# Queries and keys on all partitions in a width-one attention, and large products in two waits at its entry

## The reference

```python
    x = x + _L1_xattn_ref(_layernorm(x, axis=-1), ctx_1024, ...)
    x = x + _L1_ffn_ref(_layernorm(x, axis=-1), ...)
    x = x + _L2_attn_ref(_layernorm(x, axis=-1), L2_attn_w_qkv, L2_attn_w_out)
...
def _L2_attn_ref(x, w_qkv, w_out):
    DIM_HEADS = 64
    b, n, _ = x.shape
    h = DIM_HEADS
    qkv = jnp.einsum('bnc,fc->bnf', x, w_qkv)
    q, k, v = jnp.split(qkv, 3, axis=-1)
    q = q.transpose(0, 2, 1)[..., None]
    k = k.transpose(0, 2, 1)[..., None]
    v = v.transpose(0, 2, 1)[..., None]
    scale = 1.0 / jnp.sqrt(jnp.float32(h))
    dots = jnp.einsum('bhid,bhjd->bhij', q, k) * scale
    causal = jnp.tril(jnp.ones((n, n), dtype=bool))
    dots = jnp.where(causal, dots, -jnp.inf)
    attn = jax.nn.softmax(dots, axis=-1)
    out = jnp.einsum('bhij,bhjd->bhid', attn, v)
    out = out[..., 0].transpose(0, 2, 1)
    return jnp.einsum('bnh,ch->bnc', out, w_out)
```

## Time and profile before

| | |
|---|---|
| median of 3 runs | 3169.06 us (3167.29 to 3172.32) |
| the profiled execution | 3174.21 us, span 3172.4 us |
| TensorE busy | 2943.1 us, 93% |
| VectorE, ScalarE, GpSimd busy | 1863.2, 1253.7, 432.8 us |
| DMA | 37.75 MB, mean 12 GB/s |
| width-one stage, first scores to last values | about 1757 to 2032 us |
| mean granted clock of TensorE | 0.967 |

### The profile page before, as it was taken

How to read it: one execution, slowest core, us unless ns; L and a number is a source line. 1 busy time by engine, 2 the same in 40 slices (tenths; PEclk the granted TensorE clock), 3 DMA queues, 4 the chain that set the end, 5 groups by cost and what they waited for, 6 DMA issues and landing times.

```text
span 3172.4 us, 52215 instructions
## 1 busy us (share of the span) xinstructions
PE 2943.1 (93%) x20631; PEld 1958.4 (62%) x20671; DVE 1863.2 (59%) x6438; ACT 1253.7 (40%) x1944; POOL 432.8 (14%) x458
## 2 busy tenths in 40 slices
PE   7999999988989889988998899999999999998998
PEld 4666666865555556655655556566667766766653
DVE  5534443699999537775677788584343344434455
ACT  2222221335656433324443578554232333323443
POOL 0010010114343311000000256310000000000000
PEclk9999999998999999999999799899999999998999
DMA  3000000010000100000000111100000000000000
GB/s 129 1 1 0 1 0 1 1 52 1 2 1 2 34 32 1 1 5 1 2 1 1 27 36 26 44 2 27 1 1 1 1 1 1 1 1 9 2 1 27
DMA packets 22028, 37.75 MB, mean 12 GB/s; under 512 B 2132, under 2 KB 19733, under 8 KB 20760
## 3 DMA queue, kind: packets, MB, share of 16 engines
q1 hardware_dynamic: 20968, 34.02, 3.2%
q10 hardware_dynamic: 816, 0.39, 0.1%
HBM read 26.81 MB, written 2.10 MB: 9 GB/s over the span
## 4 chain that ended last, share of the span: by engine, by line
PE 77%; DVE 16%; ACT 4%; issue 2%; DMA 0%; DVEq 0%; SPq 0%; POOL 0%; ACTq 0%; POOLq 0%
PE ps L415 45%; DVE arena L568 4%; PE ps L620 2%; PE ps L3040 2%; PE ps L3059 2%; PE ps L686 2%; PE ps L516 2%; ACT arena L674 2%; PE ps L2356 2%; PE ps L1590 2%; PE ps L2310 2%; PE ps L727 2%; DVE arena L1924 2%; PE ps L2913 1%; PE ps L553 1%
## 5 line engine op out<-in xcount | busy, mean ns | idle before, releaser
L415 PE MATMUL ps<-weights,arena 128*128 128x256 f32 (+4 forms) x2480 | 696.1, 430 | 38.9 <-DVE arena L1805 23.5
L415 PEld LDWEIGHTS ps<-weights,arena 128*128 128x128 f32 (+1 forms) x2480 | 462.8, 196 | 204.0 <-issue 94.3
L415 PE MATMUL ps<-arena,weights 128*128 128x256 f32 (+4 forms) x1726 | 560.4, 473 | 14.5 <-DMA weights<-in_w_L_attn 5.8
L415 PEld LDWEIGHTS ps<-arena,weights 128*128 128x128 f32 (+1 forms) x1726 | 316.7, 191 | 217.7 <-issue 154.0
L415 PE MATMUL ps<-arena 128*128 128x256 f32 (+4 forms) x1618 | 429.1, 418 | 6.0 <-ACT arena L4758 1.5
L415 PEld LDWEIGHTS ps<-arena 128*128 128x128 f32 (+2 forms) x1618 | 300.1, 189 | 115.6 <-issue 74.9
L568 DVE TENSOR_REDUCE arena<-ps 128x16 f32<-128x1232 f32 (+2 forms) x96 | 179.1, 1865 | 145.4 <-PE ps L546 48.0
L674 ACT ACTIVATE arena<-ps 77x2048 f32<-77x2048 f32 (+1 forms) x112 | 210.0, 1875 | 120.2 <-PE ps L620 58.4
L1924 DVE MATCH_REPLACE8 arena<-arena 128x77 f32<-128x77 f32 x1024 | 214.3, 224 | 0.0
L2323 ACT ACTIVATE arena<-ps 128x1536 f32<-128x1536 f32 x128 | 185.7, 1451 | 56.6 <-PE ps L2312 49.7
L855 POOL TENSOR_TENSOR x<-x,weights 128x512 f32<-128x512 f32 x32 | 43.8, 1370 | 1201.0 <-DVE arena L821 1153.3
(11 more groups left out here) (427 smaller groups left out, 4421.5 us busy)
## 6 DMA issues: line engine op xcount, KB each, us to landing
arena<-arena SPq DMA_DIRECT2D x156, 32.0 KB
weights<-in_w_L_ffn SPq DMA_DIRECT2D x1, 3848.0 KB, 11.6
weights<-in_w_L_attn SPq DMA_DIRECT2D x1, 3840.0 KB, 14.8
weights<-in_w_L_xattn SPq DMA_DIRECT2D x3, 1024.0 KB, 6.3
weights<-in_w_L_ffn SPq DMA_DIRECT2D x1, 3072.0 KB, 9.9
x<-in_x SPq DMA_DIRECT2D x2, 1024.0 KB
weights<-in_w_L_xattn SPq DMA_DIRECT2D x1, 2048.0 KB, 7.5
out<-x SPq DMA_DIRECT2D x8, 256.0 KB, 2.2
```

The lines of the kernel that those rows point to most:

```text
L415: ins = k.nc.tensor.matmul(out, lhsT, rhs, start=start and i == 0, stop=i == n - 1)
```

## The change

Three things change.

Queries and keys of a batch stand on all 128 partitions: queries on 0 to 63, keys on 64 to 127, 256 columns each, where both stood on 0 to 63 side by side. The bound (which stood behind them on 64 partitions) is laid on both halves, 128 queries each. All operations that cut into parts are therefore 128x384 and not 64x768, the copy from PSUM is 128x256 and not 64x512, the minimum of the bound is written by two operations. For the bound rows there are two transfers a part and not one, so a batch has 24 and not 21; for the first batch the upper half is SyncE's.

The product itself stays in two pieces of 64 columns of weights for batches 0 to 4, the second now written to partitions 64 to 127, and becomes one of 128 columns from batch 5 on (APART). The steps of the bound are put at groups 9, 13, 13, 14, 15 from round 2 on, and not at 9, 10, 13, 13, 14.

TensorE gets nine products of 128x512 in float32 that nothing reads (`awake_tensor`): four in the last step of L1_xattn into bank 2, ahead of the transposed scores, and five in round 0 at g == 2 into bank 0, behind a wait for the exponential of group 1 and ahead of the wait for `left`'s means.

```diff
--- before.py
+++ after.py
@@ -727,6 +727,12 @@
             ins = k.nc.tensor.transpose(out[:, (2 * c + t) * P:(2 * c + t + 1) * P], src[:, t, c * P:(c + 1) * P],
                                         k.ident[:, :])
     return ins
+
+
+def awake_tensor(k, b, n):
+
+    for _ in range(n):
+        k.nc.tensor.matmul(k.ps[:, b, :], k.ctxT[:, 0, 0:P], k.ctxT[:, 0, 0:512], start=True, stop=True)
 
 
 def flat(tile):
@@ -1175,6 +1181,8 @@
                 after(pe, s, soon, "zT")
             if p in quant:
                 experts(pe, s, quant[p], "zT")
+            if p == ends:
+                awake_tensor(k, 2, 4)
             turned_first_tensor(k, pe, s, now, 3)
         if p == ends:
             step_z_tensor(k, pe, one, 1, 3)
@@ -2231,7 +2239,7 @@
 GROUPS = NH1 // 4
 PARTS = 3
 PAIRS = PARTS * PARTS
-ROWS_DMAS = 2 * PAIRS + PARTS
+ROWS_DMAS = 2 * PAIRS + 2 * PARTS
 LAG, PROBS = 3, 5
 
 
@@ -2239,15 +2247,15 @@
     st = "L2_attn"
     c, low, mid = (Carve(k.arena, k.arena_size, at) for at in (UPPER, 0, HALF))
     two = (0, 1)
-    s = Bag(stage=st, z=c.take(2, D), zT=[c.take(KC, SEQ) for _ in two], parts=c.take(PARTS, 3, SEQ, dt=BF16),
-            qkm=c.take(3, SEQ), rest=c.take(3, SEQ), v=[c.take(2, NH1) for _ in two], seen=c.take(P),
+    s = Bag(stage=st, z=c.take(2, D), zT=[c.take(KC, SEQ) for _ in two], parts=c.take(PARTS, SEQ + P, dt=BF16),
+            qkm=c.take(SEQ + P), rest=c.take(SEQ + P), kmax=c.take(SEQ), kmin=c.take(SEQ), gap=c.take(832),
+            v=[c.take(2, NH1) for _ in two], seen=c.take(P),
             krows=[c.take(16, SEQ, dt=BF16) for _ in two],
             prob=[u.take(4 * (SEQ + P)) for u in (low, low, low, low, mid)], v1=low.take(2, NH1, PAD),
             blank=[u.take(8 * SEQ) for u in (c, low)], raw=low.take(SEQ), o=low.take(2, NH1), rec=mid.take(2, NH1),
             oT=mid.take(SEQ), norms=norms_plan(k, st, TILES // 2))
     s.qrows = [rows.bitcast(BF16).rearrange("p (h q) -> p h q", h=16) for rows in s.blank]
     assert low.at <= HALF, low.at
-    s.kmax, s.kmin = s.rest[:, 0, :], s.rest[:, 1, :]
     s.sig = Signals(k.signals, st, B, 1, z=1, zT_ps=1, zT=1, qk_ps=1, qk=1, v_ps=1, v=1, put=2, parts=PARTS, s_ps=GROUPS,
                     prob=GROUPS, first=GROUPS, second=GROUPS, pv=GROUPS, raw=1, back_ps=1, rec=1, o=1, oT_ps=1, oT=1,
                     out_ps=1, done=1, stats=1, split=5)
@@ -2270,15 +2278,18 @@
 def rows_of_part(k, s, eng, n, i, queues):
 
     rows = s.moved.sems["rows"][0]
-    part, qrows, krows = s.parts[0:NH1, i], s.qrows[n % 2], s.krows[n % 2]
+    qrows, krows = s.qrows[n % 2], s.krows[n % 2]
+    q, key = s.parts[0:NH1, i, 0:SEQ], s.parts[NH1:P, i, 0:SEQ]
     eng.wait_ge(*s.sig.at("parts", 0, n, i + 1))
     for j in range(PARTS):
         if "k" in queues:
-            eng.dma_start(krows[PARTS * i + j:P:PAD, :, :], part[:, 1, :]).then_inc(rows, 16)
+            eng.dma_start(krows[PARTS * i + j:P:PAD, :, :], key).then_inc(rows, 16)
         if "q" in queues:
-            eng.dma_start(qrows[PARTS * j + i:P:PAD, :, :], part[:, 0, :]).then_inc(rows, 16)
-    if "q" in queues:
-        eng.dma_start(qrows[PAIRS + i:P:PAD, :, :], part[:, 2, :]).then_inc(rows, 16)
+            eng.dma_start(qrows[PARTS * j + i:P:PAD, :, :], q).then_inc(rows, 16)
+    for half in (0, 1):
+        if "qk"[half] in queues:
+            eng.dma_start(qrows[PAIRS + i:P:PAD, :, half * P:(half + 1) * P],
+                          s.parts[half * NH1:(half + 1) * NH1, i, SEQ:SEQ + P]).then_inc(rows, 16)
 
 
 def L2_attn_sync(k, sp, s, first, last):
@@ -2371,9 +2382,9 @@
 
 def step_qk_tensor(k, pe, s, n, b):
     pe.wait_ge(*s.sig.at("zT", 0, n, 1))
-    for i in (0, 1):
-        ins = proj_feature(k, k.ps[0:NH1, b, i * SEQ:(i + 1) * SEQ], w_of(k, s.stage, "wqkv", KC), s.zT[n % 2],
-                           i * NH1, NH1)
+    w, wide = w_of(k, s.stage, "wqkv", KC), NH1 if n < APART else P
+    for at in range(0, P, wide):
+        ins = proj_feature(k, k.ps[at:at + wide, b, 0:SEQ], w, s.zT[n % 2], at, wide)
     ins.then_inc(*s.sig.up("qk_ps"))
 
 
@@ -2430,6 +2441,8 @@
             if n == 0 and g == 0:
                 pair_back_tensor(k, pe, x, left, 6)
             if n == 0 and g == 2:
+                pe.wait_ge(*s.sig.at("prob", 0, 0, 2))
+                awake_tensor(k, 0, 5)
                 after(pe, x, left, "o")
                 fp8_turn_tensor(k, pe, x, older, 7)
             if n == 0 and g == 3:
@@ -2484,7 +2497,7 @@
 
 def step_qk_scalar(k, act, s, n, b):
     act.wait_ge(*s.sig.at("qk_ps", 0, n, 1))
-    k.nc.scalar.activation(s.qkm[0:NH1, 0:2, :], cut(k.ps[0:NH1, b, :], c=2), ACT.Copy).then_inc(*s.sig.up("qk"))
+    k.nc.scalar.activation(s.qkm[:, 0:SEQ], k.ps[:, b, 0:SEQ], ACT.Copy).then_inc(*s.sig.up("qk"))
 
 
 def step_v_scalar(k, act, s, n, b):
@@ -2539,13 +2552,13 @@
     dve.wait_ge(*s.sig.at("qk_ps", 0, n, 1))
     if n:
         dve.wait_ge(*s.sig.at("parts", 0, n - 1, PARTS))
-    v.tensor_copy(s.qkm[0:NH1, 0:2, :], cut(k.ps[0:NH1, b, :], c=2)).then_inc(*s.sig.up("qk"))
+    v.tensor_copy(s.qkm[:, 0:SEQ], k.ps[:, b, 0:SEQ]).then_inc(*s.sig.up("qk"))
 
 
 def step_bound_vector(k, dve, s, n, i):
 
     v, done = k.nc.vector, s.sig.up("split")
-    q, key, out = (s.qkm[0:NH1, j, :] for j in range(3))
+    q, key = s.qkm[0:NH1, 0:SEQ], s.qkm[NH1:P, 0:SEQ]
     kmax, kmin = s.kmax[0:NH1], s.kmin[0:NH1]
     if i == 0:
         dve.wait_ge(*s.sig.at("qk", 0, n, 1))
@@ -2559,13 +2572,16 @@
         v.scalar_tensor_tensor(kmin, q, -1.0, kmin, ALU.mult, ALU.mult).then_inc(*done)
     else:
         dve.wait_ge(*s.sig.at("split", 0, n, 2))
-        v.tensor_tensor(out, kmax, kmin, ALU.min).then_inc(*done)
+        for half in (0, 1):
+            at = slice(half * P, (half + 1) * P)
+            ins = v.tensor_tensor(s.qkm[half * NH1:(half + 1) * NH1, SEQ:SEQ + P], kmax[:, at], kmin[:, at], ALU.min)
+        ins.then_inc(*done)
 
 
 def step_split_vector(k, dve, s, n, i):
 
     v, done, part = k.nc.vector, s.sig.up("split"), s.sig.up("parts")
-    x, rest, parts = s.qkm[0:NH1], s.rest[0:NH1], s.parts[0:NH1]
+    x, rest, parts = s.qkm, s.rest, s.parts
     if i == 0:
         dve.wait_ge(*s.sig.at("split", 0, n, 3))
         if n:
@@ -2618,7 +2634,8 @@
         .then_inc(*s.sig.up("done"))
 
 
-BOUND_AT = (9, 10, 13, 13, 14)
+APART = 5
+BOUND_AT = (9, 13, 13, 14, 15)
 BOUND_LATE, BOUND_NEXT = (13, 13, 14, 14, 14), (9, 11, 13, 13, 14)
```

## The result

The changed kernel is slower. Its median is 3204.9 us in 9 runs (3182.1 to 3240.5) beside 3169.96 us for the kernel before in 9 runs (3167.3 to 3175.4). 3162 us with a range of 3152 to 3172 was forecast. The profiled execution took 3190.23 us, its span 3188.3 us, at a mean granted clock of 0.964; that of before took 3174.21 and 3172.4 at 0.967. It is 15 us shorter than the median; the executions at the median have a mean clock of 0.958, so they spend more time at half clock. Where they do is not shown, for none of them was profiled.

The account below looks back on a forecast made before the run. TensorE was taken as the bound through most of the width-one attention, with waits and half clock at the entry. Gains of 4.2 (entry) and 2.7 (one product for two) made 6.9 us, so a median of 3162 us, range 3152 to 3172.

Parts of the forecast that it names:

- The gap at 1806.1 and the half clock behind it: Second batch: TensorE's 1.7 us gap, from VectorE's backlog, and 20.4 us at half clock behind it, both left unchanged.
- the second pair: Projection of the first five batches: second pair of matmuls on the array's other columns, 0 to 0.2 us a batch, taken as nothing.
- The entry: Entry up to the output projection's end: through at 1777.8 against 1781.9 to 1782.0, 4.2 us gained.
- the first four: Four large products in the entry's first wait: 3.45 us at full clock, to 1739.8, the next row 0.65 us late.
- The second exponential: Entry, ScalarE: starts at 1745.1 against 1746.33, 1.2 us gained, with row transfers and first scores following it.
- The second set: Five large products in the entry's second wait, from 1761.5: 5.4 us, beginning at half clock and ending at full.
- Groups 3 to 6: Entry, behind the five products: full clock, value products 1.56 us apart against 2.82 at half.
- One product for two: Batches 5, 6 and 7: two matmuls of 128 weight columns replace four of 64, 2.7 us gained in all.
- VectorE and DMA: Per batch: VectorE 1.3 us less, hidden, worth 0 to 0.5; 24 transfers take 14.5 us against 12.7, also hidden.
- (a): Rival: the second batch's half clock goes too, about 6 us more gained, 3156 us; chance 0.22.
- (b): Rival: entry nets nothing, the clock falling again in groups 3 to 6; 3165.5 to 3166.5 us; chance 0.19.
- (c): Rival: slower, with half clock under both sets of products in the entry, 6.8 us later, 3175.9 us; chance 0.14.

Follow-up runs that it names:

- e3: Kernel after plus one large product ahead of the projection of queries and keys of batches 3 and 4 (rounds 1 and 2); 3169.53 us, ratio 0.9999.
- e5: Kernel after without the nine products, the projection of batches 3 and 4 made twice as one product of 128 columns; 3167.54 us, ratio 0.9972.
- e8: Kernel before, old layout, with the keys' half of the projection left out from batch 2 on; median 3205.06 us over all twelve, ratio 1.005.
- e1: Kernel before plus the nine large products and their wait, layout and transfers as before; 3170.51 us, ratio 1.0005.
- e2: Kernel after without the nine large products and their wait, so the new layout alone; 3206.32 us, ratio 1.0112.
- e7: e5 plus three large products in each of round 1's two waits for VectorE; 3161.28 us, ratio 0.9954.
- e12: The same kernel as e7, timed again; 3160.3 us, ratio 0.9951.
- e10: Kernel before, old layout and long projection, plus two large products in each of round 1's two waits; 3183.69 us, ratio 1.0011.
- e4: Kernel after plus three large products in the gap of round 1, ahead of the second batch's first values; 3180.74 us, ratio 1.0031.
- e9: e7 without the doubled projections: both waits of round 1 filled, short projection in every round; 3197.94 us, ratio 1.0063.
- e11: e7 plus one more large product at group 13 of round 1, behind that group's exponential; 3166.46 us, ratio 0.9971.

## Why the prediction was wrong

It was wrong in sign: 3162 forecast, 3204.9 measured, outside the range.

**The step that failed** is the sentence under the sum: "The gap at 1806.1 and the half clock behind it stay in this sum". The gap grew from 1.7 to 2.9 us, and the half clock behind it did not stay at 20.4 us: it lasted 71.3 us in the profiled execution and cost 18.4 us there (7.0 + 11.4). Under it lies a term taken at nothing: "the second pair goes to the other half of the array's columns: between nothing and 0.2 us a batch, taken as nothing". It was 0.85 us a batch (1.94 to 1.09), in the direction of a gain, and outside its own bound, and it shortened the block that ended the half clock. The rows pointed there: the prediction itself noted that the clock came back 1.5 us after 1827.07, inside the very block that the change shortens. They do not give the failure by themselves, for the short block still lasts 1.98 us at half clock; that took the runs. I took a block that ended the half clock as work whose only price is its length. e3 and e5 give back the length of the block and the loss is gone; e8 shortens the block alone and the loss is there.

**The entry.** Forecast 4.2 us gained, measured from the common start 1.8 lost (projection's end 72.16 us behind VectorE's marker, 70.33 before); e1 has the same (72.28). The four profiles with the nine products lie at 72.16 to 72.80 and the ten without them at 69.83 to 72.05, in both layouts, so it goes with the products and not with the layout, and part of the 1.8 is scatter. Term by term, with the 1.6 us of later arrival taken off: the first four took 5.21 us and not 3.45, since part of them ran at half. The second exponential was expected 1.2 us sooner; it starts 34.71 us behind the marker, 34.67 before. So do the first scores (45.47 and 45.46), where the wait for DMA is now 3.71 us. The second set thus starts 1.9 us later than forecast and takes 6.16 us and not 5.4, inside the bounds given. The exponential of group 3 is then at 1773.95. Groups 3 to 6 are at full clock as forecast, but TensorE waits 3.16 us for VectorE's copy (L2660), 1.55 later than the two delays explain. In that wait the clock falls, so the projection takes 3.67 us and not 1.9. 1.9 + 0.8 + 1.55 + 1.75 = 6.0 is the distance from 4.2 gained to 1.8 lost. ScalarE and VectorE of after, in the same stretch:

```profile
1771.65 0.60 ACT L1085 ACTIVATE arena<-ps 128x512 bf16<-128x512 f32 x1 [5.35 <-PE ps L727]
1772.15 1.90 ACT L1241 ACTIVATE arena<-ident 128x2048 f32<-128x2048 f32 x1
1773.95 5.46 ACT L2334 ACTIVATE arena<-ps 128x1536 f32<-128x1536 f32 x4
```

```profile
1775.42 0.69 DVE L2343 TENSOR_TENSOR arena<-arena 128x512 f32<-128x512 f32 x1 [6.43 <-ACT arena L2334]
1779.24 0.35 DVE L2589 CAST arena<-arena 128x384 bf16<-128x384 f32 x1
1781.05 0.68 DVE L2660 COPY arena<-ps 128x512 f32<-128x512 f32 x1
```

The turn of the older batch stands behind the five products, ScalarE's copy of it waits 5.35 us, and all exponentials stand behind that copy; VectorE then idles 6.43 us and has masks, bound and parts of the next batch in a row ahead of the copy that TensorE needs. The forecast had only a mask and the copy in that chain.

**One product for two.** Forecast 2.7 us. Rounds 3 to 5 take 29.45, 29.54 and 29.44 us for 30.25, 30.35 and 30.26: 0.8 each, 2.4 in all. Right, "rounds 3 to 5 shorter by 0.9 each" too, but it isn't the product count that gives it, since the side-by-side form has it as well.

**VectorE and DMA.** Forecast 1.3 us less on VectorE per batch; a cast of a part is now 0.36 and a subtraction 0.56 us, the cutting 2.20 us for 3.56. The size was right. "Hidden" was right for the half clock stretch, but the gap of round 1 is VectorE's, and it grew from 1.7 to 2.95 us: TensorE comes 0.8 us sooner, and VectorE ends it 0.4 us later in the new layout (26.2 us behind the entry's output projection in after and e2, 25.8 in before and e1). The prediction priced the gap as untouched. The 24 transfers cost nothing that a run shows.

**The rivals.** (a), the half clock of the second batch gone, did not come by itself, but e7 shows its size: from the end of the entry's output projection to the first output projection of the loop it takes 56.0 us, 61.7 before. That is 5.7 less, as (a) had it, though here by added products. The 0.49% of e12 (some 15 us) is more than the 9.1 us that its profile gains from the marker to the last output projection; the rest is not placed. (b), nothing net from the entry, has its size in e1 (1.0005), but not its mechanism: groups 3 to 6 kept the full clock, and it fell in the wait behind them. (c) had the right sign by the wrong mechanism: it wanted the nine products at half clock, of which only part was, and e1 says that they cost nothing overall.

The Trainium skill's rule (the clock released by how busy the array has been, "TensorE: Matmul & The Clock Gate", Part 1) is contradicted more strongly now than in the prediction: 142.00 busy of 142.00 us at 0.50 in e2. What the engine did in these stretches were mostly score products of depth 32 and value products of 32 columns of weights. I held the trace against the rule in one place and did not ask what, then, ended the half clock elsewhere.

**Open.** A short block is followed by the full clock in eight cases and not in eight (three of these are e8's), with no difference that I can read from the rows. That this is why executions of the kernel after differ by 58 us is likely and not shown. Why e10 fell behind a long block, and what brings more or less half clock ahead of the marker, are open too.

## What to carry to other kernels

Before making a block of dense TensorE work shorter, look at the granted clock on both sides of it: if the clock rises inside the block, the block may be what brings it up, as here, and its length is then worth far more than its time. Making it longer and shorter by itself shows it (e5, e8). A gap filled or a stretch sped up moves the wait to the next place where the slower engine is late, so a filling is priced with the wait behind it (e4, e9), and with all that stands behind it on its own engine (the entry). Time the parts of a change apart: here the layout cost 1.1% and the products nothing, and repeating two projections made the same layout 0.3% faster than before. And where executions scatter ahead of the changed stretch, measure from a row at its start to one at its end (e11 beside e12).

## What the runs showed of the hardware

- Two float32 products with 64 columns of weights, the results on PSUM partitions 0 to 63 and 64 to 127, run side by side: eight rows in 1.09 us for 1.94, without any other change.
- TensorE can stay at 1.2 GHz for 71, 142 and 160 us while it is busy the whole time, mostly with score products of depth 32 and value products of 32 columns, with projection blocks of up to 2.1 us between (after, e2, e8); the same kind of work keeps 2.4 GHz for as long once it has it (e5, 154.5 us with 151.80 busy).
- Less work can take longer: e8 leaves half of a projection out, and is 0.5% slower (1.0028 to 1.0072).
